# A decoder layer with a delta-rule scan: pairs of tokens folded in the solve, the norms' seed in PSUM, and quantile searches by quarters

## What is computed

```
# 1. delta-rule attention, 16 heads of 16 features, over x normed twice
k = k / max(norm(k), 1e-6)
step: retrieval = S k_t ; S += beta_t * (v_t - retrieval) k_t^T ; o_t = S q_t
x = x + (normed_x + out @ w_out + b_out)
# 2. cross attention to a context of 512 tokens, masked, then a layer norm
x = x + layernorm(softmax(q ctx^T / 16, masked) ctx) * gamma + beta
# 3. FFN 256 -> 1024 -> 256, int8 activations, ternary weights
def quant_act(x): amax = quantile(|x|, 0.995); s = 127 / amax; q = clip(round(x * s), -128, 127) / s
x = x + ternary(w2) @ quant_act(gelu(ternary(w1) @ quant_act(layernorm(x))))
```

## Time and profile before

| | |
|---|---|
| median of 3 runs | 1209.48 us (1209.47, 1209.48, 1211.79) |
| profiled execution | 1210.13 us, its span 1208.4 us |
| busy of the span | PE 947.1 us (78%), DVE 999.9 us (83%), ACT 632.2 us (52%), POOL 438.6 us (36%) |
| mean granted PE clock | 0.899 of full speed |

### The profile page before, as it was taken

How to read it: one execution, slowest core, us unless ns; L and a number is a source line. 1 busy time by engine, 2 the same in 40 slices (tenths; PEclk the granted TensorE clock), 3 DMA queues, 4 the chain that set the end, 5 groups by cost and what they waited for, 6 DMA issues and landing times.

```text
span 1208.4 us, 19595 instructions
## 1 busy us (share of the span) xinstructions
PE 947.1 (78%) x6080; PEld 707.4 (59%) x6087; DVE 999.9 (83%) x3021; ACT 632.2 (52%) x1476; POOL 438.6 (36%) x647
## 2 busy tenths in 40 slices
PE   1468999999999999999999998899887601794156
PEld 1357777777777777777777776666655400341034
DVE  3578999999999999999999998855666788798877
ACT  1244555555555655655556553446476440684097
POOL 2413543535435445354353441314467640000000
PEclk9688999999999999999999998899998955797579
DMA  9430000000000000000000000133300000000012
GB/s 198 59 105 1 9 7 6 10 6 7 9 5 10 6 6 10 6 9 7 6 10 5 8 8 5 27 110 105 93 13 1 1 0 0 1 1 1 1 49 92
DMA packets 30263, 30.51 MB, mean 25 GB/s; under 512 B 7248, under 2 KB 25552, under 8 KB 30160
## 3 DMA queue, kind: packets, MB, share of 16 engines
q1 hardware_dynamic: 30160, 29.26, 9.5%
HBM read 20.85 MB, written 4.19 MB: 21 GB/s over the span
## 4 chain that ended last, share of the span: by engine, by line
DVE 61%; PE 24%; issue 9%; ACT 4%; POOL 1%; DMA 1%; DVEq 0%; SPq 0%; ACTq 0%; POOLq 0%
PE ps L1543 6%; DVE arena L993 6%; DVE arena L996 6%; DVE work L1477 4%; DVE arena L975 4%; DVE arena L974 4%; PE ps L1705 3%; DVE arena L984 3%; DVE arena L987 3%; DVE arena L1039 3%; PE psY L1726 3%; DVE work L901 2%; DVE arena L1046 2%; PE psX L1726 2%; DVE arena L997 2%
## 5 line engine op out<-in xcount | busy, mean ns | idle before, releaser
L482 POOL TENSOR_TENSOR arena<-arena 128x256 f32<-128x256 f32 x32 | 23.3, 728 | 367.2 <-DVE arena L975 367.2
L572 ACT ACTIVATE arena<-ps 128x512 f32<-128x512 f32 x128 | 72.9, 596 | 49.2 <-PE ps L1601 48.7
L537 ACT ACTIVATE arena<-ps,nparity 32x256 f32<-32x256 f32 x124 | 51.1, 457 | 81.8 <-PE ps L1543 81.4
L457 POOL TENSOR_SCALAR_AFFINE_SELECT arena<-arena 128x2048 f32<-128x2048 f32 x32 | 92.1, 2877 | 2.2
L1601 PE MATMUL ps<-work 32*128 32x256 f32 x512 | 91.8, 400 | 0.8 <-ACT w2t L642 0.7
L1543 PE MATMUL ps<-work,arena 128*128 128x64 f32 x496 | 68.1, 295 | 30.6 <-DVE work L1008 30.0
L1543 PEld LDWEIGHTS ps<-work,arena 128*128 128x128 f32 x496 | 63.4, 207 | 37.7 <-DVE work L1008 37.7
L1566 PE MATMUL psG<-arena 128*128 128x512 f32 x128 | 73.8, 659 | 1.9 <-DVE arena L1039 1.9
L468 POOL TENSOR_TENSOR work<-work 128x16 f32<-128x16 f32 x96 | 51.2, 533 | 58.1 <-DVEq L1068 53.1
L1601 PEld LDWEIGHTS ps<-work 32*128 32x128 f32 x512 | 61.1, 184 | 17.5 <-issue 10.1
L993 DVE TENSOR_TENSOR arena<-arena 128x256 f32<-128x256 f32 (+1 forms) x96 | 66.4, 692 | 3.3
(11 more groups left out here) (294 smaller groups left out, 2640.2 us busy)
## 6 DMA issues: line engine op xcount, KB each, us to landing
arena<-in_mask_BxSxS_ik SPq DMA_DIRECT2D x8, 1024.0 KB, 6.7
arena<-in_x SPq DMA_DIRECT2D x32, 128.0 KB, 11.9
arena<-in_ctx SPq DMA_DIRECT2D x8, 512.0 KB, 4.2
xs<-arena SPq DMA_DIRECT2D x256, 16.0 KB, 1.8
out<-xs SPq DMA_DIRECT2D x32, 128.0 KB, 1.7
arena<-in_L_ffn_w SPq DMA_DIRECT2D x2, 1024.0 KB, 8.8
arena<-in_L_attn_w_qkvb SPq DMA_DIRECT2D x1, 1024.0 KB, 8.8
work<-in_L_attn_w_out SPq DMA_DIRECT2D x1, 256.0 KB, 4.7
```

The costliest lines, as they stand in the source:

```text
L457: G.affine_select(out=pairs, in_=pairs, compare_op=ALU.is_ge, fill=0.0, base=0, pattern=[[0, NH], [-CT, B], [0, CT]], channel_multiplier=1 ...
L572: A.activation(attn[j % 2][:, r * 512:(r + 1) * 512], ps[(2, 0)[r % 2]][:, :], ACT.Copy).then_inc(att_out, 1)
```

## The change

Three edits are joined.

*The scan's solve.* Tokens 3, 7, 11 and 15 are no longer solved on their own. `scale_near` computes one more column of G3 (the coefficient of the second token of a pair on the first) and adds to the second row of G3 its first row times that coefficient (a product with a wait, an addition without). The reduction at tokens 2, 6, 10, 14 then yields both tokens of the pair. The semaphore `u_done` comes from the reduction of token 14.

*The norms' seed.* key_norms keeps the squares in PSUM, copies them to SBUF for POOL, shifts them from PSUM to PSUM, and writes only the finished seed to SBUF.

*The searches.* Each round counts three edges at the quarters of the interval instead of one at its middle; the rounds go from 18 and 17 to 5 and 4. The first search then stops at an interval of 256 units in the last place, and finds the two wanted values by sorting: the two largest below its upper end of each partition are transposed into one row, the eight largest of the row are taken, and the places are picked by comparing with 1 to 8. The second search now runs on the values before gelu, which are integers there; its last edge is the value itself. Gelu is applied on ACT to the two values found (`two`, `two_g`), and the 2048-column gelu goes.

```diff
                 for t in range(1, CT):
+                    if t % 4 == 3:
+                        continue
                     if t % 2:
                         own(V.tensor_tensor(red[:, 0:NH], g4h[:, :, t // 2], C16[:, :, t - 1], ALU.mult))
...
-                V.tensor_tensor(G4, psG[:, 768:896], bt.rearrange("p (q t) -> p q t", t=2)[:, :, 1],
-                                ALU.mult).then_inc(pre2, 1)
+                own.issue(V.tensor_tensor(G4, psG[:, 768:896], bt.rearrange("p (q t) -> p q t", t=2)[:, :, 1], ALU.mult))
+                odd = "p (q a) -> p q a"
+                V.tensor_tensor(g3[:, :, 1, 2], psG[:, 768:896].rearrange(odd, a=2)[:, :, 1],
+                                bt.rearrange("p (q t) -> p q t", t=4)[:, :, 3], ALU.mult).then_inc(pre2, 1)
+                v.wait_ge(pre2, m + 1)
+                own.need(own.k)
+
+                folded = red[:, 0:2 * NH * 4].rearrange("p (q s) -> p q s", s=2)
+                own(V.tensor_tensor(folded, g3[:, :, 0, 0:2],
+                                    G4.rearrange("p (q a b) -> p q a b", a=2, b=1)[:, :, 1].broadcast_to([P, NH * 4, 2]), ALU.mult))
+                own.issue(V.tensor_tensor(g3[:, :, 1, 0:2], g3[:, :, 1, 0:2], folded, ALU.add))
...
-                own(V.tensor_scalar(ss, ps[1][:, 0:NH], -1.0, NORM_EPS * NORM_EPS, ALU.mult, ALU.max))
-                seed(root, ss)
+                squares, half = ps[1][:, 0:NH], ps[1][:, NH:2 * NH]
+                own(V.tensor_scalar(squares, squares, -1.0, NORM_EPS * NORM_EPS, ALU.mult, ALU.max))
+                own.issue(V.tensor_copy(ss, squares))
+                own(V.tensor_scalar(half.bitcast(I32), squares.bitcast(I32), 1, None, ALU.logical_shift_right))
+                own(V.tensor_scalar(root.bitcast(I32), half.bitcast(I32), -1.0, SEED, ALU.mult, ALU.add))
...
+                own.issue(V.tensor_tensor(quarter0, bounds[:, 1:2], bounds[:, 0:1], ALU.subtract))
+                own.need(own.k)
+                for e in range(3):
+                    done = own.issue(V.tensor_scalar(quarter[0][:, e:e + 1], quarter0, 0.25, None, ALU.mult))
                 own.need(done)
+                own(V.tensor_scalar(trial[0], places[:, 0:3], quarter[0][:, 0:1], bounds[:, 0:1], ALU.mult, ALU.add))
...
+                for r in range(ROUNDS[k]):
+                    q, q_next = quarter[r % 2], quarter[1 - r % 2]
+                    low = bounds[:, 0:1] if r == 0 else lower[r % 2]
+                    last = r + 1 == ROUNDS[k]
+                    for e in range(3):
+                        V.tensor_scalar(marks[e][:, 0:n_kept], kept_k, trial[r % 2][:, e:e + 1], None, ALU.is_ge, ALU.add,
+                                        accum_out=shares[:, e:e + 1]).then_inc(part[k], 1)
...
+                        own(V.tensor_scalar(q_next, q, 0.25, None, ALU.mult))
+                        own.issue(V.tensor_scalar(base3, places[:, 0:3], q_next[:, 0:1], low, ALU.mult, ALU.add))
...
+                    own(V.tensor_scalar(fits, psX[:, 0:3], wanted, None, ALU.is_ge, ALU.add, accum_out=passed))
...
+                        own.issue(V.scalar_tensor_tensor(lower[1 - r % 2], q[:, 0:1], passed, low, ALU.mult, ALU.add))
+                        own(V.scalar_tensor_tensor(trial[1 - r % 2], q, passed, base3, ALU.mult, ALU.add))
...
+            def in_last_block(k, kept_k):
+                n_kept = kept_k.shape[1]
+                V.tensor_scalar(marks[0][:, 0:n_kept], kept_k, upper, None, ALU.is_ge, ALU.add,
+                                accum_out=shares[:, 0:1]).then_inc(part[k], 1)
+                own(V.scalar_tensor_tensor(cand2[:, 0:n_kept], kept_k, upper, kept_k, ALU.is_lt, ALU.mult))
+                own(V.max(tops, cand2[:, 0:n_kept]))
+                V.tensor_tensor(top2[:, 1:2], top2[:, 1:2], tops[:, 2:3], ALU.max).then_inc(part[k], 1)
+                v.wait_ge(whole[k], 3 + ROUNDS[k])
+                own.issue(V.tensor_scalar(place[0:1, :], psX[0:1, 3 * P:3 * P + 1], -1.0, wanted[0:1, :], ALU.mult, ALU.add))
+                own.issue(V.max(in_order, psX[0:1, 0:2 * P]))
+                own(V.tensor_reduce(row3[0:1, 2:3], psX[0:1, 2 * P:3 * P], AX.X, ALU.max))
+                own.issue(V.scalar_tensor_tensor(at_place[:, 0, :], places[0:1, :], place[0:1, :], in_order, ALU.is_equal, ALU.mult))
+                own(V.scalar_tensor_tensor(at_place[:, 1, :], low_places[0:1, :], place[0:1, :], in_order, ALU.is_equal, ALU.mult))
+                V.tensor_reduce(row3[0:1, 0:2], at_place, AX.X, ALU.max).then_inc(part[k], 1)
...
+                own(V.tensor_copy(two[:, 1:2], psX[:, 0:1]))
+                V.copy_predicated(two[:, 1:2], keep_i, two[:, 0:1]).then_inc(found, 1)
+                v.wait_ge(found, 1)
+                own(V.tensor_tensor(flag[:, k:k + 1], psX[:, 1:2], two[:, 1:2], ALU.is_ge))
+                v.wait_ge(cand_ready, 1)
...
-            A.activation(cand, cand, ACT.Gelu, scale=deq[:, 0:1]).then_inc(cand_ready, 1)
+            act.wait_ge(found, 1)
+            A.activation(two_g, two, ACT.Gelu, scale=deq[:, 0:1]).then_inc(cand_ready, 1)
...
-            v.wait_ge(cand_ready, 1)
+            v.wait_ge(picked, NT * 2)
             own.restart()
             quantile(1, g, NT * FF, NT * FF // SEG * 8, 0.1875)
```

More of the change, by code:

```diff
@@ L236, in decoder @@
         spare = take_work(NT * FF // SEG * 2)
-        kept, ranks = spare[:, 0:256], spare[:, 320:384]
-        marks = spare[:, 256:320].bitcast(mybir.dt.uint8)
-        ones_b = spare[:, 384:384 + P // 2].bitcast(BF16)
+        kept, ranks, ones_b = spare[:, 0:256], spare[:, 256:320], spare[:, 320:384].bitcast(BF16)
         edge_marks = cand2.bitcast(mybir.dt.uint8)
-        own_at = [448]
+        marks = [edge_marks[:, 4096 + 256 * e:4352 + 256 * e] for e in range(3)]
+        spare_at = [384]
         def a_few(n, dt=F32):
-            own_at[0] += n
-            return spare[:, own_at[0] - n:own_at[0]].bitcast(dt)
-        counts, steps, chosen, bounds = a_few(EDGES), a_few(EDGES + 1), a_few(3 * EDGES), a_few(3)
-        chosen = chosen.rearrange("p (a n) -> p a n", a=3)
+            spare_at[0] += n
+            assert spare_at[0] <= NT * FF // SEG * 2
+            return spare[:, spare_at[0] - n:spare_at[0]].bitcast(dt)
+        counts, steps, bounds, tops = a_few(EDGES), a_few(EDGES + 1), a_few(3), a_few(8)
+        chosen = a_few(3 * EDGES).rearrange("p (a n) -> p a n", a=3)
         edge_i = a_few(EDGES + 1, I32)
         edge = edge_i.bitcast(F32)
-        share = a_few(1, BF16)[:, 0:1]
-        wanted, outside, guess, guess_f = (a_few(1) for _ in range(4))
+        shares = a_few(2, BF16)
+        places, low_places, in_order = a_few(8), a_few(8), a_few(8)[0:1, :]
+        at_place = a_few(16)[0:1, :].rearrange("p (a n) -> p a n", a=2)
+        wanted, outside, guess, guess_f, passed, place, upper, quarter0 = (a_few(1) for _ in range(8))
+        lower = [a_few(1) for _ in range(2)]
+        quarter = [a_few(3) for _ in range(2)]
+        trial = [a_few(3) for _ in range(2)]
+        two, two_g = a_few(2), a_few(2)
+        base3, fits, row3 = a_few(3), a_few(3), a_few(3)
         guess_i = a_few(1, I32)
@@ L986, in solve @@
                                             ALU.mult))
-                        own(V.tensor_reduce(C16[:, :, t:t + 2], part, AX.X, ALU.add))
+                        last = V.tensor_reduce(C16[:, :, t:t + 2], part, AX.X, ALU.add)
+                        if t == CT - 2:
+                            last.then_inc(u_done, 1)
+                            v.wait_ge(u_done, j + 1)
+                        else:
+                            own(last)
                     else:
@@ L1341, in narrowed @@
                     own.issue(V.memset(ones_b, 1.0))
-                for e in range(EDGES + 1):
-                    done = own.issue(V.memset(steps[:, e:e + 1], float((e - 1) << BLOCK[k])))
-                own.need(done)
+                    for e in range(8):
+                        done = own.issue(V.memset(places[:, e:e + 1], e + 1.0))
+                    own.need(done)
+                    own.issue(V.tensor_scalar(low_places, places, float(hi - lo), None, ALU.add))
+                own(V.tensor_scalar(steps, places[:, 0:EDGES + 1], -2.0, float(1 << BLOCK[k]), ALU.add, ALU.mult))
                 v.wait_ge(whole[k], 1)
@@ L1391, in narrowed @@
                                                          ALU.is_ge, ALU.max))
-                    elif r == 4:
+                    if r + 1 == ROUNDS[k]:
+                        own.need(own.k)
                         own.issue(V.scalar_tensor_tensor(top2[:, 1:2], outside, 3.0e38, top2[:, 1:2], ALU.mult, ALU.max))
                     own.need(own.k)
-                    if r + 1 < BLOCK[k]:
-                        own(V.tensor_tensor(next_i, c_i, after, ALU.bitwise_xor))
                     v.wait_ge(whole[k], 3 + r)
-                    own(V.scalar_tensor_tensor(drop_i, psX[:, 0:1], wanted, bit, ALU.is_lt, ALU.mult))
```

84 lines of the change are left out of this document (46 added, 38 removed).

## The result

The changed kernel takes 1139.37 us, the median of four runs (1137.56 to 1141.53), against 1210.63 us for the kernel before on the same chip. The ratio is 0.9404, with a 95% interval from 0.9368 to 0.944. The prediction was 1141.1 us. The profiled execution took 1137.68 us, with a span of 1135.8; it lies 1.7 us under the median.

The account below looks back on a forecast made before the run. It took DVE (VectorE) to bound the scan, with PE some 6% behind. The profiled 1210.13 us less 44.2 (scan) and 24.2 (searches) gave 1141.7, less 0.65 to the median 1141.1; range 1134 to 1156.

Parts of the forecast that it names:

- The bound passes to PE: Scan: DVE's loop drops from 21.82 to 19.73 us, so PE becomes late and a chunk takes 20.40.
- -1.76: Scan's solve: four odd tokens lose their multiply and add, 4 x 0.44 us off DVE's loop.
- +0.75: scale_near: one more 64-element product, a folded product with its wait and an add lengthen DVE's loop, bounds 0.6 and 1.2.
- -1.08: Norms' seed: from 1.86 us to 0.78 with the shift in PSUM, no longer stalled beside POOL's select.
- PE's floor: Scan: chunk less PE's waits of 0.93 and 0.20 and 0.16 overlap for each, 20.37 us, taken as 20.40.
- The wait for POOL at L1587: Scan: PE's 0.20 us wait goes because POOL's norms start about 0.9 us earlier; otherwise the floor is 20.73.
- The searches: 2.6 us too good: Both searches: rounds of 1.63 and 2.24 us, with finishes and the shorter gelu, together save 24.2 us.
- (1) The clock's drops: Scan: drops to half clock cost about 1.7 us each with PE as bound, +13.6, giving 1155; chance 0.10.
- (2) The stall moved: Norms' seed: stall moves to another seed operation, DVE's loop is 20.9 us, giving 1155; chance 0.08.
- (3) PE is the bound: Scan: the rival held that PE isn't the bound, a chunk takes 19.73 us, giving 1123; chance 0.06.
- (4) The slow branch: Searches: a set flag makes DVE and PE run the full bisection, giving about 4000 us; chance 0.03.
- (5) The folding shortens the solve: Solve: the rival held that folding doesn't shorten it, as its reduce waits longer, giving about 1173 us; chance 0.03.

Follow-up runs that it names:

- less work for VectorE: The changed kernel without the folded product and its addition in scale_near, so part of the solve's coefficients is left out: 1134.07 us.
- more work for VectorE: The changed kernel with the solve's widest reduction done twice, 1.25 us more on VectorE in each chunk, same result: 1185.35 us.

## Why the prediction was right, point by point

**The bound passes to PE: right, and closer than told.** The chain's shares, the chunk with less work for VectorE and the wait at L1077 show it. But the prediction took VectorE's loop to be 19.73 us, 0.67 under PE. It is 20.18. The sum of its terms (-1.76, +0.75, -1.08) came out as -1.76, +0.84 and -1.03, which gives 19.87; what it lacked is the new stall of L991, +0.29, which makes 20.16 of the 20.18. No row of before showed it, since the norms' wide product fell elsewhere. It didn't cost anything, as PE's 20.22 came first by 0.04, and that was luck: the prediction had no term for a collision outside the seed. One of its own signs shows the miss: L1056 (now L1077) was to wait about 0.9 us for PE, and waits 0.35; only without the folded product, with 0.89, is it as told.

**PE's floor: the step that was mis-sized.** Forecast 20.37, taken 20.40; measured 20.22, or 1.61 less per chunk instead of 1.42, and under the 20.30 that was the least allowed for. The waits that go are 0.93 and 0.20, as read, and each gives back the overlap of 0.16 that was taken: from start to start, L1736 and L1618 are 0.25 apart (1.34 before), L1641 and L1662 0.96 (1.33). What the sum lacked is that the instructions behind a wait are themselves slower: from L1618 to the gram behind it, L1635, it is 1.73 (1.84 before), and from L1662 to the next L1676 0.31 (0.36). The four make 1.62. Over 27 chunks the miss of 0.19 is 5.1 of the 6.8 us by which the scan is better than forecast. The wait for POOL at L1587 went, as argued: L484 ends at 334.29 and PE comes at 334.50. But POOL's chain is still held once, at its sixth operation (1.08 us) where the prediction had it free.

**The searches: 2.6 us too good.** A round takes 1.83 to 1.90 us in the first search (the last 1.58) against 1.63, and 2.44 to 2.56 in the second (the last 2.18) against 2.24. Two terms were short. From the last accumulator read to the use of PE's sum it is 0.59 and not 0.50, because L1417 with two operands by partition takes 0.29 (operations of three columns take 0.16 with none, as L1416, and 0.22 with one, as L1439). The compare and the two operations after it take 0.66 and not 0.52: the compare's accumulator read stands before them, and L1438 and L1439 are 0.22 each. The rounds alone are 9.0 and 9.6 us against 8.2 and 9.0. That is 1.4 of the 2.6; 0.6 lies in the stage of the first FFN product, 0.2 at the end, and 0.4 before and after the rounds. The misses of scan and searches had opposite signs, so the total of 1141.1 is closer than its parts. Profiled execution against profiled execution 1141.7 was forecast and 1137.68 came, 4.0 less; that the median lies 1.7 above this execution brings the two numbers closer still. Both are luck.

**Rivals.** (1) The clock's drops: none in the middle chunks of after, and none in those of the kernels where PE waits 0.69 us or less for VectorE (the seed alone 0.69, the folding alone 0.23, the select left out 0.24). They are there where that wait is 0.93 to 0.96 (before, the searches alone, more work for VectorE). This is what goes together in these kernels; no run varied that wait by itself, step by step. A drop with PE as the bound occurred in no middle chunk, so its price of 1.7 us was not tested; with VectorE as the bound and without the shift's cover it is 0.4 to 0.7. (2) The stall moved, but not within the seed: into the solve, 0.35 with the seed alone and 0.29 in the whole change. The mechanism was half right and its place wrong. (3) PE is the bound. (4) The slow branch wasn't taken: the searches take 26 and 37 us. (5) The folding shortens the solve as told.

## What to carry to other kernels

When an engine's loop is shortened, ask where every instruction of VectorE with two SBUF operands will now lie against GpSimd's instructions: the stall removed at one place can come back at another, and here it decided how much the parts were worth alone and together. A floor made of busy time and removed waits was good to some 0.2 us in 20 here; two engines that come out nearer than that can't be told apart by such a sum, and an edit to one of them alone moved the chunk by 0.05 us at most. In a chain of one-column operations, cost each new operation by its own form: operands by partition and accumulator reads were the two terms too small.

## What the runs showed of the hardware

- Shifts, copies and products of 16 columns with their source in PSUM, whether they write PSUM or SBUF, take VectorE 0.17 to 0.18 us each beside a running GpSimd select, as short as the same shift in SBUF with nothing beside it (0.174 in the earlier trace rows).
- The contention works in both directions. In the kernel after, POOL's 16-column product takes 1.08 us where it takes 0.22 otherwise, since VectorE's L1060 of two SBUF operands (330.41, 1.23) had started before it; the two end at 331.72 and 331.64:

```profile
330.33 0.24 POOL L477 TENSOR_TENSOR work<-work 128x16 f32<-128x16 f32 x1
330.64 1.08 POOL L478 TENSOR_TENSOR work<-work 128x16 f32<-128x16 f32 x1
```

- A period of two chunks can arise from a collision: 19.60 and 20.58 us by turns over the whole scan, with the same instructions in each. A mean over chunks, or a look at a single one, would not have shown it.
